# A decoder layer on one core: the exponentials of two score tiles in one instruction, and the low part and the first body reordered

## The reference

```python
x = x + attn(layernorm(x))            # causal, 32 query heads of 16, 8 key/value heads
x = x + xattn(layernorm(x), ctx_4096) # below
x = x + ffn(layernorm(x))             # x @ kernel + bias + two low-rank terms
# xattn(Q, K): 16 heads, latent of 32
C_q = Q @ Wq_d; C_kv = K @ Wkv_d
scores = einsum('bnhl,bkl->bhnk', (C_q @ W_qk).reshape(b, n, 16, 32), C_kv) / sqrt(32)
out = einsum('bhnk,bkhd->bnhd', softmax(scores), (C_kv @ Wv_u).reshape(b, nkv, 16, 32))
```

## Time and profile before

| | us |
|---|---|
| median of three runs | 624.7 |
| the profiled execution | 625.17 |
| its span in the trace | 623.4 |
| TensorE busy (matmul) | 575.0, 92% of the span |
| GpSimd busy | 424.6, 68% |
| VectorE busy | 404.1, 65% |
| ScalarE busy | 324.6, 52%, 680 instructions |

### The profile page before, as it was taken

How to read it: one execution, slowest core, us unless ns; L and a number is a source line. 1 busy time by engine, 2 the same in 40 slices (tenths; PEclk the granted TensorE clock), 3 DMA queues, 4 the chain that set the end, 5 groups by cost and what they waited for, 6 DMA issues and landing times.

```text
span 623.4 us, 11522 instructions
## 1 busy us (share of the span) xinstructions
PE 575.0 (92%) x4104; PEld 314.5 (50%) x4104; DVE 404.1 (65%) x703; ACT 324.6 (52%) x680; POOL 424.6 (68%) x414
## 2 busy tenths in 40 slices
PE   7887797999999999999999999999999999998876
PEld 6435353645456445645555544645565454444444
DVE  2627673697657766796758766795858764647562
ACT  1522345457554745567544745466635745464571
POOL 6202386789787878688786978788786977688000
PEclk9997898899999999999999999999999999799899
DMA  8959711606142351607051441617060522100000
GB/s 324 412 121 359 252 25 29 231 20 236 29 150 126 85 197 32 243 24 257 11 192 77 135 149 41 235 29 253 19 233 17 198 76 61 37 11 1 24 2 16
DMA packets 31579, 77.40 MB, mean 124 GB/s; under 512 B 11297, under 2 KB 24961, under 8 KB 29218
## 3 DMA queue, kind: packets, MB, share of 16 engines
q1 hardware_dynamic: 30854, 75.27, 36.0%
q10 hardware_dynamic: 668, 1.40, 0.6%
HBM read 58.92 MB, written 2.88 MB: 99 GB/s over the span
## 4 chain that ended last, share of the span: by engine, by line
PE 64%; DVE 18%; SPq 5%; DMA 4%; ACT 3%; issue 2%; POOL 2%; ACTq 0%; POOLq 0%; DVEq 0%
PE st_ps L774 11%; PE mx_ps L823 11%; PE pv_ps L789 10%; DVE mx_p L1255 5%; PE mi_ps L548 4%; PE mi_ps L536 4%; SPq L434 3%; PE mi_ps L752 2%; PE mi_ps L645 2%; DVE p L1216 2%; PE mi_ps L649 2%; DMA ctx_sb<-in_ctx_t 2%; PE mi_ps L756 2%; PE mi_ps L555 2%; PE mi_ps L612 2%
## 5 line engine op out<-in xcount | busy, mean ns | idle before, releaser
L1326 POOL TENSOR_TENSOR acc<-acc,p_ring 125x448 f32<-125x448 f32 x290 | 348.2, 1201 | 76.1 <-ACT p_ring L1030 40.2
L1255 DVE TENSOR_REDUCE mx_p<-mx_ps 128x1 f32<-128x500 f32 x336 | 210.6, 671 | 104.5 <-PE mx_ps L823 103.3
L1030 ACT ACTIVATE p_ring<-st_ps 125x448 f32<-125x448 f32 x372 | 184.5, 545 | 135.5 <-PE st_ps L774 130.0
L774 PE MATMUL st_ps<-q_st,c_st 98*125 98x448 f32 x372 | 148.0, 433 | 3.0 <-ACT p_ring L1030 2.8
L823 PE MATMUL mx_ps<-c_st,q_st 96*128 96x500 f32 x336 | 140.2, 451 | 9.7 <-DVE mx_p L1255 3.9
L774 PEld LDWEIGHTS st_ps<-q_st,c_st 98*125 98x125 f32 x372 | 66.4, 192 | 94.7 <-ACT p_ring L1030 75.4
L789 PE MATMUL pv_ps<-p_ring,c_nat 125*32 125x448 f32 x768 | 95.1, 568 | 4.2 <-ACT p_ring L1030 2.2
L823 PEld LDWEIGHTS mx_ps<-c_st,q_st 96*128 96x128 f32 x336 | 63.3, 197 | 39.0 <-DVE mx_p L1255 18.1
L1334 POOL TENSOR_TENSOR rstd<-mv,eps_col 128x1 f32<-128x1 f32 x24 | 4.9, 206 | 74.9 <-DVE mv L1109 74.4
L555 PE MATMUL mi_ps<-ctx_sb,wkv_sb 128*32 128x375 f32 x480 | 42.6, 493 | 2.0 <-DVE p L1164 2.0
L1326 POOL TENSOR_TENSOR acc<-p_ring 125x448 f32<-125x448 f32 x29 | 33.9, 1169 | 5.3 <-ACT p_ring L1030 5.3
(11 more groups left out here) (145 smaller groups left out, 669.7 us busy)
## 6 DMA issues: line engine op xcount, KB each, us to landing
ctx_sb<-in_ctx_t SPq DMA_DIRECT2D x16, 3000.0 KB, 11.6
c_st<-ct_hl SPq DMA_DIRECT2D x192, 46.9 KB, 3.5
q_st<-q_hl SPq DMA_DIRECT2D x90, 56.0 KB, 2.0
x_sb<-in_x SPq DMA_DIRECT2D x8, 256.0 KB, 2.8
out_y<-x3n SPq DMA_DIRECT2D x16, 112.0 KB
wq_sb<-in_wq SPq DMA_DIRECT2D x2, 512.0 KB, 6.3
kern_sb<-in_lora_a SPq DMA_DIRECT2D x1, 1024.0 KB, 14.3
wo_sb<-in_wo SPq DMA_DIRECT2D x1, 1024.0 KB, 17.9
```

Source lines behind the costliest of these rows:

```text
L774: mm(st_bank(unit)[0:KC, 0:HALF], c_st[:, b % 4, t * KT + k * KC:t * KT + (k + 1) * KC], q_st[:, b // 2 % 2, b % 2, half * HALF:(half + 1) ...
L1030: act.activation(p_ring[:, unit % PR, :], st_bank(unit)[0:KC, 0:HALF], ACT.Exp, scale=float(L) ** -0.5).then_inc(exp_done, 1)
L1255: ve.tensor_reduce(mx_p[:, p:p + 1], mx_ps[unit % MXB][:, 0:KP], AX.X, ALU.max).then_inc(red_done, 1)
L1326: po.tensor_tensor(dst, first, p_ring[:, unit % PR, :].rearrange("p (h s) -> p h s", s=S), ALU.add).then_inc(acc_done, 1)
```

## The change

Four things.

- The exponentials of units u and u+1 (u even) become one instruction, `exponentials`, over 2 x 448 columns in two neighbouring PSUM banks, which are now allocated as one tensor (`st_two`; `mx_two` for two of the maxima's banks). It waits for both scores and for the ring's two slots. The score of either unit waits for the whole pair before it; in batch 15 for the pair before that.
- In `STEPS`, group 3, the step `SM1` becomes `SX1` (maximum of the rows) ahead of `AS`, and `SS1` (subtraction) behind it.
- In `FIRST_STEPS`, group 3: `SB` ahead of a maximum and `NM`. Group 9: `CT` of the batch ahead of `T2` (the transposes of the normalised rows).
- The two DMAs of `spread_m` for batch 1 are issued by SP, in its order of steps, and no longer by ScalarE.

```diff
@@ -87,7 +87,7 @@
     [("Qh", "n"), ("M", 3), ("Q1", "n"), ("M", 2)],
     [("M", 1), ("WA", "n"), ("SA", "n")],
     [("SX0", "n"), ("WB", "n"), ("SB", "n"), ("SS0", "n"), ("M", 3), ("Ah", "a"), ("SE0", "n"), ("A", "a"),
-     ("NM", "m"), ("SM1", "n"), ("AS", "a")],
+     ("NM", "m"), ("SX1", "n"), ("AS", "a"), ("SS1", "n")],
     [("MT", "m"), ("V", "n"), ("CT", "a"), ("SN0", "n")],
     [("Ah", "b"), ("A", "b"), ("SN1", "n"), ("AS", "b")],
     [("P0", "n"), ("M", 1), ("P1", "n"), ("M", 1), ("P2", "n"), ("P3", "n"), ("XC", "f"), ("M", 1)],
@@ -107,12 +107,12 @@
 FIRST_STEPS = {0: [("Ah", "a"), ("M", 2), ("L0", "n"), ("M", 1), ("A", "a")],
                1: [("AS", "a"), ("CT", "a"), ("M", 1), ("T1", "n")],
                2: [("K", "n"), ("M", 1), ("Qh", "n"), ("M", 3), ("Q1", "n")],
-               3: [("WA", "n"), ("M", 1), ("SA", "n"), ("M", 2), ("WB", "n"), ("M", 1), ("NM", "m"), ("SB", "n"),
+               3: [("WA", "n"), ("M", 1), ("SA", "n"), ("M", 2), ("WB", "n"), ("SB", "n"), ("M", 1), ("NM", "m"),
                    ("SM0", "n"), ("SM1", "n")],
                4: [("Ah", "b"), ("MT", "m"), ("SE0", "n"), ("A", "b"), ("AS", "b"), ("SE1", "n"), ("V", "n"),
                    ("SN0", "n")],
                5: [("SN1", "n")],
-               9: STEPS[9] + [("NM", "o")], 10: [("MT", "o"), ("L0", "x")], 11: []}
+               9: [("CT", "b"), ("M", 1), ("T2", "n"), ("M", 1), ("CQ", "n"), ("M", 1), ("H", "n"), ("NM", "o")], 10: [("MT", "o"), ("L0", "x")], 11: []}
 ALONE_STEPS = {0: [("Ah", "a"), ("M", 2), ("A", "a"), ("M", 1)], 1: [("AS", "a"), ("CT", "a"), ("M", 5)], 2: [("M", 1)],
                3: [("M", 3), ("NM", "m")], 4: [("MT", "m")], 5: []}
 
@@ -270,8 +270,11 @@
                     acc[0:64, :, :, :].rearrange("p a h s -> p (a h s)")]
 
 
-        st_ps = [bank(f"st_ps{n}") for n in range(STB)]
-        mx_ps = [bank(f"mx_ps{n}") for n in range(MXB)]
+        st_two = stack.enter_context(nc.psum_tensor("st_two", [128, 2, 512], F32))
+        mx_one = bank("mx_ps0")
+        mx_two = stack.enter_context(nc.psum_tensor("mx_two", [128, 2, 512], F32))
+        st_ps = [st_two[:, n, :] for n in range(STB)]
+        mx_ps = [mx_one[:, :], mx_two[:, 0, :], mx_two[:, 1, :]]
         pv_ps = bank("pv_ps")
         mi_ps = [bank(f"mi_ps{n}") for n in range(2)]
 
@@ -508,7 +511,7 @@
                             if n % 2 and n + 2 < B:
                                 load_ctx(n + 2)
                         elif name == "MT":
-                            if n in (0, B - 2) or (n % 2 and n > 1):
+                            if n in (0, B - 2) or n % 2:
                                 sp.wait_ge(mt_sb, n + 1)
                                 spread_m(dma, n)
                             if n % 2 and n + 1 < B:
@@ -768,9 +771,9 @@
                 if b == B - 1 and g == 0 and t == 2:
                     pe.wait_ge(red_done, B * PIECES)
                 if b == B - 1 and (g or t > 1):
-                    pe.wait_ge(exp_done, unit - 3)
+                    pe.wait_ge(exp_done, unit - unit % 2 - 2)
                 elif unit >= STB:
-                    pe.wait_ge(exp_done, unit - STB + 1)
+                    pe.wait_ge(exp_done, unit - unit % 2)
                 mm(st_bank(unit)[0:KC, 0:HALF], c_st[:, b % 4, t * KT + k * KC:t * KT + (k + 1) * KC],
                    q_st[:, b // 2 % 2, b % 2, half * HALF:(half + 1) * HALF],
                    start=True, stop=True).then_inc(st_done, 1)
@@ -996,10 +999,6 @@
                     if n:
                         act.wait_ge(m_in[(n - 1) % 2], 32 * ((n - 1) // 2 + 1))
                     copy(m_t[:, :], o[0:2 * ROWT, 0:128]).then_inc(mt_sb, 1)
-                    if n == 1:
-
-                        act.wait_ge(mt_sb, n + 1)
-                        spread_m(act.dma_start, n)
                 elif name == "Y":
 
                     copy(y_t[:, :, :].rearrange("p q (b s) -> p q b s", b=2)[:, :, :, 0:S],
@@ -1012,13 +1011,14 @@
                 elif name == "F1":
                     copy(ax_t[0:2 * RANK, :], o[0:2 * RANK, 0:128]).then_inc(f1_sb, 1)
 
-            def exponential(b, g, t):
+            def exponentials(b, g, t):
+
                 unit = b * 24 + g * 4 + t
                 if unit == 0:
 
                     act.wait_ge(eff_out, 32)
-                act.wait_ge(st_done, unit + 1)
-                old = unit - PR
+                act.wait_ge(st_done, unit + 2)
+                old = unit + 1 - PR
 
                 if old >= 0:
                     act.wait_ge(pv_done, old // 4 + 1)
@@ -1027,8 +1027,9 @@
                         act.wait_ge(acc_dve, dve_adds(*added) + max(old % 12, 1))
                     else:
                         act.wait_ge(acc_done, pool_adds(*added) + max(old % 12, 1))
-                act.activation(p_ring[:, unit % PR, :], st_bank(unit)[0:KC, 0:HALF], ACT.Exp,
-                               scale=float(L) ** -0.5).then_inc(exp_done, 1)
+                two = mx_two if unit >= (B - 1) * 24 and unit % 4 else st_two
+                act.activation(p_ring[:, unit % PR:unit % PR + 2, :], two[0:KC, :, 0:HALF], ACT.Exp,
+                               scale=float(L) ** -0.5).then_inc(exp_done, 2)
 
             def out_of_sums(b, half):
                 act.wait_ge(pv_done, b * 6 + half * KG + KG)
@@ -1079,8 +1080,8 @@
                     part, gg = g // GROUPS, g % GROUPS
                     bs = 2 * i - 1 + part
                     for t in range(4):
-                        if 0 <= bs < B:
-                            exponential(bs, gg, t)
+                        if 0 <= bs < B and t % 2:
+                            exponentials(bs, gg, t - 1)
                         for name, n in between(i, g, t):
                             step(name, n)
                     bl, gl = (bs, gg - 1) if gg else (bs - 1, GROUPS - 1)
@@ -1139,7 +1140,7 @@
                         .then_inc(a_lo, 1)
                 elif name == "NM":
                     negated_maxima(n)
-                elif name in ("SM0", "SM1", "SX0", "SS0"):
+                elif name in ("SM0", "SM1", "SX0", "SS0", "SX1", "SS1"):
                     if name[1] in "MX":
                         softmax_most(n, int(name[2]))
                     if name[1] in "MS":
```

## The result

The changed kernel took 641.9 us in the median (640.46 to 644.98, four runs) beside 625.6 us for the kernel before on the same chip (four runs): a ratio of 1.028, with an interval of 1.024 to 1.032 (the quotient of the two medians alone is 1.026). I had forecast 634 with a range of 624 to 641: the direction was right, the size was not. The profiled execution took 640.46 us with a span of 638.7, 15.3 us more than the span before; my sum for that difference was 9.2.

What follows compares the result with a forecast made beforehand. TensorE held 64% of the chain of waits, ScalarE 3%, so TensorE's waits for ScalarE count. Six bodies 5.4, first body 0.7 and last body 3.1 sum to 9.2 us on 625.17: about 634, range 624 to 641.

Steps and rivals of the forecast that it cites:

- Covered groups and groups 0, 2, 7: Pair's wait hidden where a maximum and sums stand between; exposed 0.17 us in group 0, 0.20 in 2, 0.15 in 7.
- Groups 9 to 11: Only four transposes between pairs from group 10 to 11: 0.9 us a body (0.75 to 0.95); nothing counted for group 9.
- Groups 4 to 6: Pairs lose 0.1 to 0.2 us each, ahead of waits ending with something else; nothing counted there.
- The low part: Splitting the second softmax's step removes TensorE's 0.81 us wait before the latents' transposes; gain taken as 0.5 us a body.
- The first body: Reordered steps and the second batch's maxima issued on SP: sum +0.7 us.
- (a): First body: half of the scores' masking goes ahead of the maxima's negation, latents start about 1.1 us sooner: -0.8.
- (b): First body, group 9: the latents' copy and the pair stand ahead of the copy the next product waits for: +0.8.
- (c): First body: second batch's maxima spread on SP lands at 109.2, delaying that batch's first score: +0.7 (0 to 1.4).
- rival 3: First body: spread lands in time, TensorE's clock rises, -5.4 us with the reorders; about 621, chance 0.12.
- The last body: GpSimd's additions released later +1.5, group 11's feed-forward wait +0.6, last batch's six rounds +1.0: sum +3.1 us (1 to 4).
- The covered pair: Bodies: pair's exposed time is half, 0.5 us a body, cancelling the low part's 0.5; 627, chance 0.13.
- The dearer pair: Pair takes twice a single, 1.09 us; covered groups lose 0.14 each, 1.4 us a body more; 643, chance 0.09.

Runs made afterwards that it cites:

- e11: The kernel before, unchanged, run once more for a second profile of its last body: one run, 622.3 us.
- e7: Changed kernel with ScalarE's copy of the sums in group 9 moved behind the copy of the transposed rows, bodies 1 to 6: 637.0 us, ratio 1.022.
- e1: Kernel before plus only the pair with its waits; step orders and issue of batch 1's maxima as before: 649.0 us, ratio 1.038.
- e8: Changed kernel with GpSimd's second addition in group 3 held until VectorE's first softmax subtraction is done, bodies 1 to 6: 640.2 us, ratio 1.027.
- e3: Kernel before plus only the split of the second softmax half's step, with the low part between: 621.4 us, ratio 0.9945.
- e6: Changed kernel with pairs only in groups 0, 1, 3, 7, 8 of bodies 0 to 6, single exponentials with old waits elsewhere: 626.6 us, ratio 1.0038.
- e4: Changed kernel with the pair's instruction taken apart into two of 448 columns, all of its waits kept: 644.5 us, ratio 1.031.
- e9: e3 plus the edits of e7 and e8, single exponentials throughout, measured against the kernel before: 627.7 us, ratio 1.0062.

## Why the prediction was right or wrong

**Price of the pair: right.** 0.917 us, and 0.05 from its end to the next score (348.95 to 349.00).

**Covered groups and groups 0, 2, 7: right.** Groups 1, 3 and 8 lose 0.02 or less. Groups 2 and 7 lose 0.24 and 0.15 for 0.20 and 0.15, and group 0 loses 0.18 to 0.21 in bodies 2 to 6 for 0.17.

**Groups 9 to 11: right in the sum only.** I had 0.9 for 10 and 11 and nothing for 9. They lose 0.38 (group 9), 0.29 and 0.24, together 0.91. The score that I followed behind the four transposes is 0.86 us later against the pair ahead of it, as derived. But that pair itself starts 0.56 sooner after the first score of its group than before, where TensorE had waited 0.15 us for a maximum behind VectorE's addition of 1.67 us (rows at e11). So the pair costs group 10 what I derived, and 0.56 comes back because the shift of GpSimd's additions frees an instruction that I had not looked at; that the sum came out is luck. I looked only for what the pair delays on its own bank, and not for copies behind it on ScalarE, though I had done just that in group 0. Group 9 has the same case, and e7 shows it to be worth 0.38 us.

**Groups 4 to 6: the step that failed in the bodies.** "They lose 0.1 to 0.2 each, but ahead of waits that end with something else (the low part below, the residual's sum on VectorE), so I count them there and nothing here." They lose 1.07 us a body (e1), 0.71 of it in group 4. Two things were missing. First, in group 4 ScalarE comes late to the scores, since the softmax's exponential and both copies of the latents stand ahead: the pair then runs wholly behind the second score, and some 0.3 us show, by the wait that is left in e8 (0.29). Second, the pairs shift GpSimd's additions against VectorE, so that the subtraction ahead of that exponential takes 1.93 us for 1.33: up to another 0.33 (e8 gave that back, and took away 0.85 us of lengthening, of which the pairs had added 0.60). And the wait for the low part, which was to take such losses up, hangs on the same ScalarE and VectorE work, so it moved along and grew (e1, 1.03 for 0.81).

**The low part: right by itself, wrong in this place.** 0.52 us a body on the kernel before (e3), forecast 0.5; 1.1 with the pair. I had taken the exposures of groups 4 to 6 off its 0.81 as 0.4. Net, the two gave -0.02 us a body instead of -0.5. That is 0.48 of the 0.6 between 1.50 and 0.9, over six bodies 2.9 us.

**The first body: near in size, by luck.** +0.5 for +0.7. Rows of the changed kernel, answering to the earlier trace rows:

```profile
67.51 1.47 PE L558 MATMUL mi_ps<-ctx_sb,wkv_sb 128*32 128x375 f32 x16 [0.85 <-DVE p L1165]
...
73.96 0.74 PE L777 MATMUL st_two<-q_st,c_st 98*125 98x448 f32 x1 [2.29 <-DMA q_st<-m_t]
...
99.20 0.60 PE L662 MATMUL mi_ps<-xnt,wqd_sb 128*64 128x112 f32 x8 [1.22 <-ACT xnt L913]
...
107.25 1.59 SPq L386 DMA_DIRECT2D q_st<-m_t  x2
...
110.16 0.44 PE L777 MATMUL st_two<-q_st,c_st 98*125 98x448 f32 x1 [3.21 <-DMA q_st<-m_t]
```

(a) The latents' wait fell from 2.01 to 0.85 us, but the first score then waited 2.29 for the landing of batch 0's maxima; 0.47 of it stayed, for 0.8. (b) The product of group 9 waits 1.22 us for its copy, as argued. (c) SP issued the second batch's maxima at 107.25 (forecast 106.5 and 107.3), and TensorE waited 3.21 us for the landing. The first score of the second batch came 1.6 us later than before; group 0 behind it then took 6.68 us at a granted clock of 0.74, for 7.72 at 0.62 before (7.77 at 0.62 in the second profile), and gave 1.0 back. That return is a part of what rival 3 had, and my sum had none of it. A single profile carries over 1 us of chance here: in the kernel before's second profile the first score came 2.2 us later than in its first.

**The last body: the other term that failed.** GpSimd's run began 1.4 us later against the body, as forecast, and the rounds of batch 15 are 0.19 to 0.20 us longer each, for 0.15. Rows of the changed kernel, TensorE and GpSimd:

```profile
553.21 0.74 PE L777 MATMUL st_two<-q_st,c_st 98*125 98x448 f32 x1 [0.64 <-ACT p_ring L1031]
560.91 0.68 PE L777 MATMUL st_two<-q_st,c_st 98*125 98x448 f32 x2 [0.45 <-ACT p_ring L1031]
562.64 0.68 PE L777 MATMUL st_two<-q_st,c_st 98*125 98x448 f32 x2 [0.73 <-ACT p_ring L1031]
...
566.19 0.65 PE L777 MATMUL st_two<-q_st,c_st 98*125 98x448 f32 x2 [1.15 <-ACT p_ring L1031]
...
585.89 0.19 POOL L1335 TENSOR_TENSOR rstd<-mv,eps_col 128x1 f32<-128x1 f32 x1
586.64 0.78 PE L826 MATMUL mx_ps<-c_st,q_st 96*128 96x500 f32 x1 [3.18 <-DVE mx_p L1256]
608.03 0.96 PE L792 MATMUL pv_ps<-p_ring,c_nat 125*32 125x448 f32 x8 [0.65 <-ACT p_ring L1031]
```

I had one exposed boundary, between groups 2 and 3, and then let GpSimd bind. The body has little left between its pairs in groups 2 to 9, and they wait there too: 3.3 us at full clock, for 1.5. With that TensorE reaches the transposes behind the third normalisation late enough that it no longer waits 1.34 us for GpSimd there, as it did before. Of the 5.8 us, 3.3 are these waits and 1.2 batch 15's six rounds; the rest lies in groups 10 and 11, where VectorE's addition ahead of that normalisation took 1.66 us for 0.82, beside GpSimd's additions, and TensorE's clock in groups 10 and 11 was 0.72 for 0.80. Against the second profile of before the 8.0 us are these 3.3 and 1.2, and 3.4 by which groups 2 and 3 took longer at a clock of 0.54 than in e7 at the full one (11.08 for 7.67).

**The rivals.** The covered pair (627) fell: e6 is that kernel, and it needs singles elsewhere. The dearer pair (643) has the time and not the cause: at 1.09 us each the covered groups would have lost 0.14, and they lost 0.02. The clock of the first body (621) fell with the landing at 110, not 106.5, though 1.0 us of it came. From the time alone the second rival would have been taken for the cause.

**What stays open.** In groups 2 to 6 of the last body the granted clock fell to between 0.5 and 0.65 for one or two groups in all five kernels with pairs there (the changed one, e1, e4, e7, e8), and in two of eight profiles with single exponentials (the first of before, and e9). A fall costs 1.2 us (e4) to 3.6 (the first of before). Whether the pairs' waits bring the fall about or it was chance was not settled.

## What to carry to other kernels

Joining two instructions on an engine that waits for another one buys nothing and takes the overlap of two buffers away; read, for each place, what the producer has to do meanwhile, and what already stands ahead of the joined instruction on its own engine, since there the whole length shows. A wait takes up a new delay only if what ends it doesn't hang on the same late engine: follow its chain back before a loss is put down as hidden. And what one engine does at another moment can lengthen a neighbour's instructions: a price from the trace holds only for what ran beside it. One profile is one execution: two of the same kernel differed here by 1.8 us in the same six bodies.

## What the runs showed of the hardware

A subtraction or multiplication of 128x896 on VectorE with both sources in SBUF takes 1.08 us alone. In the traces of before, after and the eleven runs 267 of them took over 1.15 us. Every one began while an instruction of GpSimd was under way (one of its additions 246 times, its own share of the softmax 21 times) and ended 0.94 to 0.96 us after that one's end. In the changed kernel's group 4 above, the addition runs from 344.32 to 345.46 and the subtraction ends at 346.41. The next addition then takes 1.82 us for 1.14. Reductions and operations that read PSUM beside the same additions kept their times (0.67 and 0.54); a cast of 7 columns from SBUF to SBUF, 0.17 us alone, took 0.60 to 0.98 beside them in the changed kernel. The Trainium skill, SBUF — State Buffer, section SBUF: two separate sides, says that VectorE and GpSimd share a pair of ports as an exclusive lock, held for a whole instruction, and that a VectorE operation with two SBUF inputs and a GpSimd operation that reads SBUF exclude each other; the trace agrees. I had not expected that lengthening one subtraction by 0.85 us would cost TensorE 0.33 us a body (e8), nor (e9) that mending one such place opens the next.
